# A two-layer transformer on one core: the last head's share of the output projection is taken straight from its strips, and the residual is added by TensorE

## The reference

```python
x = _layernorm(x + attention_0(x))      # softmax(q k^T / 4 + causal) v, heads side by side, then @ Wo + bo
x = _layernorm(x + mixture_0(x))
x = _layernorm(x + attention_1(x))      # ... @ wo.T
x = _layernorm(x + mixture_1(x))        # out.at[sel_idx].add(gelu(tok @ W1[i]) @ W2[i] * p)
```

## Time and profile before

| | us |
|---|---|
| median of 3 runs (lowest, highest) | 693.44 (691.79, 694.69) |
| profiled execution | 689.28 |
| its span, first to last instruction | 687.5 |
| PE busy | 589.1 (86%) |
| DVE busy | 518.8 (75%) |
| ACT busy | 358.8 (52%) |
| POOL busy | 183.3 (27%) |
| mean granted TensorE clock | 0.90 of full |

### The profile page before, as it was taken

The page is one execution under the profiler, slowest core; times in us unless marked ns, Lnnn a source line. Parts: engine busy times, 40 slices in busy tenths (PEclk is TensorE's granted clock), DMA queues, the critical chain, the costliest instruction groups (busy, mean ns, idle before and its releaser), DMA issues. The chain is left out here.

```text
span 687.5 us, 12671 instructions
## 1 busy us (share of the span) xinstructions
PE 589.1 (86%) x4686; PEld 403.4 (59%) x4686; DVE 518.8 (75%) x1029; ACT 358.8 (52%) x691; POOL 183.3 (27%) x296
## 2 busy tenths in 40 slices
PE   3989999996589999958989999999999857987793
PEld 2745555554467888856744444444444624976782
DVE  4788888875658766674678999999994587877636
ACT  3226777773344334342214878888888261443452
POOL 4334555562023222130500111111010000234550
PEclk9959999999589999986975999999999955998998
DMA  4534554621231211001520434424421431044331
GB/s 163 67 88 68 86 86 84 92 65 46 54 115 46 61 50 49 0 1 61 65 29 2 65 48 65 61 49 69 58 64 39 135 120 68 1 147 146 92 77 61
DMA packets 27541, 47.15 MB, mean 69 GB/s; under 512 B 13232, under 2 KB 18464, under 8 KB 26208
## 3 DMA queue, kind: packets, MB, share of 16 engines
q1 hardware_dynamic: 22112, 39.11, 27.5%
q0 software_dynamic: 4288, 7.20, 3.9%
q10 hardware_dynamic: 1088, 0.13, 0.1%
HBM read 25.22 MB, written 7.83 MB: 48 GB/s over the span
## 5 line engine op out<-in xcount | busy, mean ns | idle before, releaser
L467 ACT ACTIVATE probs<-ps 128x512 f32<-128x512 f32 x448 | 213.3, 561 | 79.2 <-PE ps L384 78.8
L360 PE MATMUL ps<-k_stack,q_stack 62*128 62x512 f32 x448 | 174.5, 466 | 7.5 <-DVE row_max L563 3.3
L384 PE MATMUL ps<-q_stack,k_stack 64*128 64x512 f32 x448 | 160.1, 435 | 9.8 <-ACT probs L467 5.9
L563 DVE TENSOR_REDUCE row_max<-ps 128x1 f32<-128x1024 f32 x128 | 149.8, 1214 | 16.2 <-PE ps L360 16.2
L384 PEld LDWEIGHTS ps<-q_stack,k_stack 64*128 64x128 f32 x448 | 76.1, 190 | 81.9 <-ACT probs L467 65.2
L399 PE MATMUL ps<-probs,v_ones 128*32 128x256 f32 (+7 forms) x2048 | 116.4, 344 | 1.9 <-ACT probs L467 1.0
L360 PEld LDWEIGHTS ps<-k_stack,q_stack 62*128 62x128 f32 x448 | 80.0, 200 | 37.6 <-DVE row_max L563 16.5
L560 DVE CUSTOM_DVE_ANT_0 y_sums<-ps,wide_mask 128x1024 f32<-128x1024 f32 (+7 forms) x128 | 91.4, 755 | 13.1 <-PE ps L360 11.8
L399 PEld LDWEIGHTS ps<-probs,v_ones 128*32 128x32 f32 x2048 | 51.5, 110 | 44.5 <-issue 14.0
L518 POOL TENSOR_SCALAR_AFFINE_SELECT probs<-probs 128x128 f32<-128x128 f32 x128 | 39.3, 313 | 46.4 <-ACT probs L467 45.1
L899 POOL TENSOR_TENSOR w_chunk_l_m<-y_sums,w_chunk_h_m 128x512 fp32r<-128x512 f32 (+1 forms) x24 | 24.3, 1039 | 101.5 <-ACT w_chunk_h_m L957 94.3
(11 more groups left out here) (208 smaller groups left out, 1125.1 us busy)
## 6 DMA issues: line engine op xcount, KB each, us to landing
y_sums<-in_w_experts SPq DMA_DIRECT2D x8, 1024.0 KB, 5.2
y_sums<-in_w_chunks SPq DMA_DIRECT2D x12, 384.0 KB, 3.1
q_stack<-part_rows SPq DMA_DIRECT2D x32, 128.0 KB, 3.4
k_stack<-part_rows SPq DMA_DIRECT2D x32, 128.0 KB, 3.9
head_sums<-sums POOLq DMA_DIRECT2D x28, 128.0 KB, 2.0
q_stack<-part_rows SPq DMA_DIRECT2D x32, 64.0 KB, 4.0
k_stack<-part_rows SPq DMA_DIRECT2D x32, 64.0 KB, 3.9
q_stack<-max_rows SPq DMA_DIRECT2D x128, 2.0 KB
```

The lines of the kernel that those rows point to most:

```text
L360: mm = pe.matmul(scores_bank(s, a, b), stack("q_stack", h, slice(0, TOP))[:, qt * P:(qt + 1) * P], stack("k_stack", h, slice(0, TOP))[:, a ...
L384: pe.matmul(bank(at % 3, 0, b - a), stack("k_stack", h, slice(0, SIDE))[:, kt * P:(kt + 1) * P], stack("q_stack", h, slice(0, SIDE))[:, a: ...
L467: act.activation(probs[:, t % 4, a:b], bank(at % 3, 0, b - a), ACT.Exp).then_inc(exp_done, 1)
L563: dve.tensor_reduce(row_max[:, h % 2, qt:qt + 1], scores_bank(s, 0, end), AX.X, ALU.max).then_inc(scores_free, 1)
```

## The change

Four things are done, the first three in both attentions.

- The last head stays where it is. Its output, divided by the sums (`own`), is multiplied strip by strip in plain fp32 by the last 16 rows of Wo (`last_raw`, loaded in place of `bias_o`, with bo as a 17th row against the row of ones that sum/sum gives). These are products of 32 rows by 32 columns of weights and 256 columns, four to a tile. The split of the last head and its four DMAs go away, and half k = 1 of `project_out` uses 112 rows.
- The residual is added by PE: x is rebuilt in the accumulator by products of `xt_l` and `xt_h` with an identity matrix (`residual`). DVE's addition goes away, as do in layer 0 the load of x by tokens and POOL's additions of the bias.
- The statistics and the normalizations read the sum in PSUM. The tail works in two halves of four tiles: residual, k = 0, k = 1, last head; the six unread products go away. SP starts the mixture's first loads as soon as the second group is split.
- In the last scatter the eight sums have a place each (four banks). They begin with x times an fp32 identity, which needs no result of the last expert, and DVE's addition goes away.

```diff
-            sp.dma_start(mem["bias_o"][:, :], dram["bias_o"].broadcast_to([P, D])).then_inc(rest_in, 16)
+            sp.dma_start(mem["last_raw"][:, :, :], dram["w_last"]).then_inc(rest_in, 16)
...
-            if not rope:
-                sp.dma_start(mem["x"][:, :, :], dram["x_tok"]).then_inc(extra_in, 16)
...
-            store_heads(sp, H - 1, range(QUADS // 2), own_step, 10)
-            if not rope:
-                sp.wait_ge(extra_in, 16)
+            sp.wait_ge(own_stored, 16 * QUADS)
             sp.wait_ge(group_low, 2)
...
+            def residual(t):
+
+                toks = slice(t * P, (t + 1) * P)
+                for k in range(KD):
+                    for part in ("xt_l", "xt_h"):
+                        pe.matmul(out_bank(t)[:, k * P:(k + 1) * P], mem[part][:, k, toks], mem["ident_r"][:, :],
+                                  start=k == 0 and part == "xt_l" and t % 2 == 0, stop=False, skip_group_check=True)
...
+                rows, toks, w = slice(0, P - k * HD), slice(t * P, (t + 1) * P), slice(k * D, (k + 1) * D)
+                product(pe, out_bank(t), (yt_h[rows, k, toks], yt_l[rows, k, toks]),
+                        (mem["wa_h"][rows, w_o, w], mem["wa_l"][rows, w_o, w]), False, False)
+
+            def project_last(t):
+
+                n, toks = (H - 1) % 2, slice(t * STRIP, (t + 1) * STRIP)
+                for c in range(QUADS):
+                    rows = slice(c * 2 * HD, (c + 1) * 2 * HD)
+                    mm = pe.matmul(out_bank(t)[rows, :], own[rows, n, toks], mem["last_raw"][rows, layer, :],
+                                   start=False, stop=True, skip_group_check=True)
+                mm.then_inc(o_ready, 1)
+
+            if not rope:
+                pe.wait_ge(ident_ready, 1)
             pe.wait_ge(scores_free, H * NT)
-            for t in range(NT):
-                project_out(t, 0)
-            for _ in range(6):
-                keep_warm(0, HALF)
-            pe.wait_ge(group_low, 2)
-            pe.wait_ge(own_stored, 2 * 16 * QUADS)
-            for t in range(NT):
-                project_out(t, 1).then_inc(o_ready, 1)
+            for g in range(2):
+                tiles = range(4 * g, 4 * g + 4)
+                for t in tiles:
+                    residual(t)
+                if g == 0:
+                    pe.wait_ge(group_low, 1)
+                for t in tiles:
+                    project_out(t, 0)
+                if g == 0:
+                    pe.wait_ge(group_low, 2)
+                    pe.wait_ge(own_stored, 16 * QUADS)
+                for t in tiles:
+                    project_out(t, 1)
+                if g == 0:
+                    pe.wait_ge(own_step, 8)
+                for t in tiles:
+                    project_last(t)
...
-            if not rope:
-
-                pool.wait_ge(extra_in, 16)
-                for t in range(NT):
-                    pool.tensor_tensor(mem["x"][:, t, :], mem["x"][:, t, :], mem["bias_o"][:, :], ALU.add).then_inc(biased, 1)
...
+                if h == H - 1:
+                    return
                 dve.wait_ge(own_step, count + 3)
...
             for t in range(NT):
                 dve.wait_ge(o_ready, t // 2 * 2 + 2)
-                dve.tensor_tensor(mem["x"][:, t, :], out_bank(t), mem["x"][:, t, :], ALU.add).then_inc(o_out, 1)
-                dve.wait_ge(o_out, t + 1)
                 norm.statistics(dve, t)
...
-                    act.activation(x[:, t, :], x[:, t, :], ACT.Identity, bias=self.shift[:, t:t + 1], scale=self.rstd[:, t:t + 1]
+                    act.activation(x[:, t, :], self.source(t), ACT.Identity, bias=self.shift[:, t:t + 1], scale=self.rstd[:, t:t + 1]
...
+            pe.wait_ge(x_back, 16)
+            pe.wait_ge(p_ready, E1)
+            pe.wait_ge(before_ready, NT * E1)
+            for t in range(NT):
+                pe.matmul(out_tile(t), consts[:, C_ID:C_ID + P], x[:, t, :], start=t % 2 == 0, stop=False, skip_group_check=True)
             pe.wait_ge(yl_ready, 1)
             pe.wait_ge(hot_t_out, NQ)
...
-            dve.wait_ge(x_back, 16)
             for t in range(NT):
-                dve.wait_ge(back_ready, t + 1)
-                dve.tensor_tensor(x[:, t, :], bank(ROW + t % 2, 0, D), x[:, t, :], ALU.add).then_inc(added, 1)
-                dve.wait_ge(added, t + 1)
+                dve.wait_ge(back_ready, t // 2 * 2 + 2)
                 norm.statistics(dve, t)
```

More of the change, by code:

```diff
@@ L473, in take_sums @@
                 act.activation(sums[:, h % 2, :], bank(7, h % 2 * (T // QUADS), T // QUADS), ACT.Copy).then_inc(sums_out, 1)
+            if not rope:
+                act.activation(mem["ident_r"][:, :], mem["consts"][:, C_ID:C_ID + P], ACT.Copy).then_inc(ident_ready, 1)
             act.wait_ge(low_ready[0], 4)
@@ L672, with __init__ @@
 class NormStage:
-    def __init__(self, nc, ctx, mem, name, first_bank=4, last=False):
+    def __init__(self, nc, ctx, mem, name, first_bank=4, last=False, source=None):
         self.mem, self.last, self.count, self.first_bank = mem, last, 0, first_bank
+        self.source = source or (lambda t: mem["x"][:, t, :])
         sb = lambda n, shape: ctx.enter_context(nc.sbuf_tensor(f"{n}_{name}", shape, F32))
@@ L1110, in mixture_1 @@
         down_ready, scaled_ready, yh_ready, yl_ready = sem("down_ready"), sem("scaled_ready"), sem("yh_ready"), sem("yl_ready")
-        back_ready, added, stored = sem("back_ready"), sem("added"), sem("stored")
+        back_ready, stored = sem("back_ready"), sem("stored")
         router = Router(nc, ctx, mem, "m1", E1, 2, ps[:, 0:2 * NT * E1], borrowed(mem, 2 * KD * H1 + KD * E1, T)[0:2 * E1, :])
         top = TopTwo(nc, ctx, mem, "m1", E1, C_T4)
-        norm = NormStage(nc, ctx, mem, "m1", last=True)
+        norm = NormStage(nc, ctx, mem, "m1", last=True, source=lambda t: out_tile(t))
         block = ctx.enter_context(nc.Block())
@@ L1131, in slot_columns, with out_tile @@
             return bank(SMALL, 16, 4 * ST).rearrange("p (s c) -> p s c", c=4)
+        def out_tile(t):
+            return bank(ROW + t // 2, t % 2 * D, D)
         def turned_piece(e, q):
@@ L1375, in _ @@
                     ranks(e + 2)
+            pe.wait_ge(x_back, 16)
[3 more added lines that the diff above has]
+                pe.matmul(out_tile(t), consts[:, C_ID:C_ID + P], x[:, t, :], start=t % 2 == 0, stop=False, skip_group_check=True)
             pe.wait_ge(yl_ready, 1)
             pe.wait_ge(hot_t_out, NQ)
-            back = [0]
             for t in range(NT):
-                if t >= 2:
-                    pe.wait_ge(added, t - 1)
-                terms = [(e, s, y) for e in back for s in range(ST) for y in y_parts]
-                for n, (e, s, y) in enumerate(terms):
-                    mm = pe.matmul(bank(ROW + t % 2, 0, D), one_hot_t[:, e, s, t * P:(t + 1) * P], y[:, e, s, :],
-                                   start=n == 0, stop=n == len(terms) - 1)
+                terms = [(s, y) for s in range(ST) for y in y_parts]
+                for n, (s, y) in enumerate(terms):
+                    mm = pe.matmul(out_tile(t), one_hot_t[:, 0, s, t * P:(t + 1) * P], y[:, 0, s, :],
+                                   start=False, stop=n == len(terms) - 1, skip_group_check=True)
                 mm.then_inc(back_ready, 1)
@@ L1533, in program @@
                 "bias_v": sb(heads, "bias_v", [P, D]),
-                "bias_o": sb(heads, "bias_o", [P, D]),
+                "last_raw": sb(heads, "last_raw", [P, 2, D]),
+                "ident_r": sb(heads, "ident_r", [P, P], F32R),
                 "wa_h": sb(heads, "wa_h", [P, 10, KD * D], F32R),
@@ L1601 @@
             wq.T, wq[swap].T, wk.T, wk[swap].T, a["L1_attn_wv"].T, a["L1_attn_wo"].T]
+    by_strip = lambda w, bias: np.tile(np.concatenate([w[D - HD:], bias.reshape(1, D), np.zeros((HD - 1, D), np.float32)]), (QUADS, 1))
+    last = [by_strip(a["L0_attn_Wo"], a["L0_attn_bo"]), by_strip(a["L1_attn_wo"].T, np.zeros(D, np.float32))]
     router0 = np.concatenate([a["L0_ffn_w_router"], a["L0_ffn_gate_w"], np.zeros((1, D), np.float32)]).T
@@ L1611 @@
         "bias_v": a["L0_attn_bv"].reshape(1, D),
-        "bias_o": a["L0_attn_bo"].reshape(1, D),
+        "w_last": np.stack(last, 1),
         "bias_g": a["L1_ffn_bg"].reshape(1, E1),
```

18 lines of the change are left out of this document (5 added, 13 removed).

## The result

| us | before | changed |
|---|---|---|
| median (lowest, highest; runs) | 692.6 (690.67, 695.59; 12) | 686.14 (682.43, 690.38; 12) |
| profiled execution | 689.28 | 686.86 |
| its span | 687.5 | 684.9 |
| mean granted clock of the profiled execution | 0.902 | 0.908 |

The ratio is 0.9908 [0.9888, 0.9928]: 0.9% faster, 6.5 us between the medians. Between the two profiled executions it is 2.4 us (2.6 in the span), because that of before lay 3.3 us under its median and that of the changed kernel 0.7 us above. So the trace shows where time goes, and the runs how much.

What follows compares the result with a forecast made beforehand. PE was taken to work nearly everywhere except in the tails, bounded by the DMA wait and then DVE's pace. Gains of 1.3 + 2.7 + 1.45 = 5.5 us off the 693.44 median gave 688.0 us, range 683.5 to 695.0.

Steps and rivals of the forecast that it cites:

- The strips' price: Last head's product in both attention tails: four 32-row strips run side by side, 0.43 us a tile.
- one after the other: Last head's strips run singly, 1.72 us a tile, about 12 us more in all, 705 us; chance 0.11.
- two at a time: Last head's strips run in pairs, 0.86 us a tile, 5.2 us more, 693.2 us, no change; chance 0.08.
- first rival: Last head's strips run singly, 705 us, chance 0.11; said to decide from about 0.9 us a tile on.
- Layer 1: Layer 1's attention tail: no DMA wait, PE becomes the bound, ACT sets the mark at 553.6 instead of 554.87, gain 1.3 us.
- Layer 0: Layer 0's attention tail: gain 3.5 us at full clock, 1.8 if half clock is granted; middle taken, 2.7.
- The scatter: Last scatter at the kernel's end: identity products run during scaling and splitting, gain 1.45 us; loss of 1.7 at 0.86 each.
- Reading PSUM: DVE's statistics and normalizations in tails and scatter: reading the sum from PSUM costs no more than from SBUF.
- dear PSUM: Reading PSUM on DVE and ACT costs more than by the rows, 0.5 us a stage, 689.6 us; chance 0.08.
- What costs nothing: Layer 0's x load, POOL's additions, unread products, identity copy, earlier weight loads: nothing; larger `last_raw` at most 0.3 us.
- handed back: Mixtures start earlier but run at half clock for longer, costing 4 us, 692 us; chance 0.07.

Runs made afterwards that it cites:

- second profile: The changed kernel run once more, unaltered, and profiled again: median 686.09 us, ratio 0.9907 to the kernel before; `own` to mark in layer 0 11.03 us.
- doubled strips: The changed kernel with every strip product of the last head issued twice: median 691.69 us, ratio 1.0002 to the kernel before.
- early order: The changed kernel with residual and half k = 0 of all eight tiles ahead of the wait for `own`: 685.22 us, ratio 0.9903 to before.
- kept busy: The changed kernel with twelve unread warming products in PE's two gaps of layer 0's tail: 686.54 us, ratio 0.9919 to before.
- the split: The changed kernel, but PE adds x only for layer 0's tiles 0 to 3, DVE elsewhere; layer 0's half k = 0 early: 679.4 us, ratio 0.9813 to before.

## Why the prediction was right

The forecast was 688.0 us in a range of 683.5 to 695.0, faster with 0.68. It is 686.14. Step by step:

- **The strips' price, right.** 0.43 us a tile with four side by side; the rivals "one after the other" and "two at a time" are out. The Trainium skill ("TensorEngine Tiling (Array Packing)", "Gotcha 1: PSUM Pressure") says that different row tiles can't access the same PSUM bank at once. These four stand in different rows of the array and write 32 partitions each of one bank, and thirty-two instructions take as long as sixteen: the measurement decides, nothing waits. The first rival's break-even was right as well: from 0.9 us a tile on it would have decided, and at 0.87 the gain was zero.
- **Layer 1, right.** Gain 1.3 forecast, 1.46 from `own` to the mark; PE is the bound and ACT sets the mark, as said.
- **Layer 0, the mis-sized term.** The prediction put "up to 1.7 us more" on half clock, for the last head's four tiles. These did take 1.7 us more (3.63 against 1.93). But residual and both halves of tiles 4 to 7 ran at half too: between the strip groups' starts lie 10.88 us mostly at half clock and 6.67 at full (172.23 to 178.90 in the second profile), so the cost is 4.2 us and the tail loses 0.5. At full clock it gains 3.7 (forecast 3.5). My middle of 2.7 stood between outcomes of -0.5 and 3.7.
- **The scatter.** Identity products at 0.43 us each and statistics 0.53 us apart (forecast 0.43 and 0.56); the mark gained 2.0 us in the profile, forecast 1.45. Half of the difference lies ahead of ACT, which starts 7.78 us behind the last expert product where 8.09 was forecast, and half behind: ACT takes four tiles in 1.93 us from PSUM where 2.07 was assumed, and the square root starts 0.1 us ahead of their end. In the runs this gain isn't seen.
- **Reading PSUM, wrong.** I took L706 on SBUF to be undoubled since it was no faster than an addition. But that addition itself already read PSUM. L724 takes 536 ns from PSUM and 406 from SBUF in the same kernel: 0.13 us a tile, 0.5 a stage. The Trainium skill ("VectorE: DVE Perf Modes", "Why PSUM operands drop a tier") had it right, and the 0.13 us a tile that the prediction worked out from it are what the trace shows. On ACT it goes the other way, 564 against 586 ns, and `bn_stats` loses nothing (400 against 428). Behind both layers' marks the half microsecond is seen: from the mark to the router's first step it is 6.14 us now and was 5.61, so that layer 1 gained only 0.93 us of its 1.46. The rival that the prediction called dear PSUM was right on DVE, at its own 0.5 us a stage.
- **What costs nothing, right.** The load and POOL's additions (684.33 with them kept). `bias_g` lands at 11.41 (issued at 4.91, 6.5 us), DVE is done at 11.49: 0.08 us of cover left of the 0.15 forecast:

```profile
bias_g<-in_bias_g SPq DMA_DIRECT2D x1, 2.0 KB, 6.5
...
4.91 0.49 SPq L102 DMA_DIRECT2D bias_g<-in_bias_g  x1
...
11.27 0.22 DVE L141 COPY wide_mask<-consts 128x128 f32<-128x128 f32 x1
```

- **Where the sum had no term.** The places give, with layer 0 at full clock, 3.7 + 1.5 - 1.0 (PSUM, both layers) + 2.0 = 6.2 us, and with half clock there 2.0; the medians say 6.5. The changed kernel's mean granted clock over its runs is 0.910 and 0.912 (12 and 6 runs), that of before 0.896 to 0.898 (24, 21 and 17 runs). Within the 62 runs of before, time goes with the time spent at half clock (correlation 0.87, 0.27 us for each us); pooled within all kernels it is 0.31. By those slopes the 20 us less of half clock (122.8 against 142.5) would be worth 5 to 6 us by themselves, so place by place and clock can't both be counted in full. The doubled strips speak for the places: that kernel has as little half clock as the changed one (120.5 us, mean clock 0.913) and is still no faster than before, and the 5.6 us that it takes longer than the changed one are those of its two tails. The prediction's fourth rival, handed back, is neither shown nor excluded: two kernels with a shorter layer 0 tail (early order, kept busy; shorter than in the changed kernel's first profile) were no faster than the changed one, within intervals of 2 to 2.5 us either way, and a third, the split, was much faster.
- **Luck.** That the forecast came within 2 us is in part luck. Layer 0's term was the middle of two outcomes 4.2 us apart, 1.0 us of PSUM was left out, and the scatter's term is in the profile but not in the times. The three runs that the gain was taken off lay 0.8 us above the median of twelve, so that of the 1.9 us between forecast and result 1.0 are gain (5.45 against 6.46).

## What to carry to other kernels

- A removed DMA wait is worth what the engine can do with the time. Put an addition on the engine that idles at that place: in the profiles x on PE was free in layer 0 before `own`, and cost 1.9 us in layer 1, where PE had become the bound (the times of these kernels lie too close to tell).
- When a price is taken from another row, ask first which memory that row's operands are in.
- Profile a kernel twice before explaining a tail by its clock: here one program showed 15.25 and 11.03 us for the same stretch.

## What was not expected of the hardware

- Four 32-row strips with one PSUM bank as target take as long as two (1.93 and 1.92 us for four tiles).
- DVE's `tensor_scalar` is 0.13 us slower from PSUM (536 against 406 ns for 256 columns), `bn_stats` 0.03 us faster (400 against 428), ACT's activation 0.02 us faster (564 against 586).
- The stretch of half clock moves between executions of one program: in the two profiles of the changed kernel the first one behind layer 0's attention began at 170.2 in one and at 183.4 in the other, with PE's gap of 1.78 us shortly ahead of the first, and ahead of the second gaps of 1.09 and 0.94 us and then one of 2.13 us that ended at 183.0.
